# Summing every second product of the first level by accumulating DMA, and a third place for B

## The reference

```python
x = x + conv_block(_gn(x))    # L0: each image makes its own 7x7 depthwise filters
x = x + ssm_block(_gn(x))     # L1: three levels of a state space model, both directions

def _ssm(x, ...):             # per level and direction, n = 16 states
    dA  = exp(delta[..., None] * A)
    dBx = delta[..., None] * Bs[:, :, None, :] * xt[..., None]
    h = h * dA + dBx                     # a scan over positions, per channel and state
    y = sum over states of h * C, + xt * Dv
    return layernorm(y, g, b)            # over the 128 channels
```

## Time and profile before

| | us |
|---|---|
| median of 3 runs | 4344.43 |
| lowest, highest | 4341.24, 4347.71 |
| the profiled execution | 4338.19 |
| its span | 4336.4 |

### The profile page before, as it was taken

How to read it: one execution, slowest core, us unless ns; L and a number is a source line. 1 busy time by engine, 2 the same in 40 slices (tenths; PEclk the granted TensorE clock), 3 DMA queues, 4 the chain that set the end, 5 groups by cost and what they waited for, 6 DMA issues and landing times.

```text
span 4336.4 us, 51200 instructions
## 1 busy us (share of the span) xinstructions
PE 3086.1 (71%) x11852; PEld 1449.5 (33%) x11852; DVE 3559.6 (82%) x4199; ACT 2552.1 (59%) x6006; POOL 3338.1 (77%) x1908
## 2 busy tenths in 40 slices
PE   6977767777776778767777876777877777876511
PEld 3433333333332433333333333333333333332200
DVE  2178888888888888888888888888888888898777
ACT  4466665655665665666656666665676566565432
POOL 0069597895969879696896969789596996969798
PEclk8988788888888888887888888888887888888755
DMA  1036354463544446354453534446253454635444
GB/s 40 1 125 206 117 179 147 157 200 108 197 140 157 165 147 204 115 190 146 157 186 125 201 129 167 149 159 209 99 196 131 168 174 137 205 113 182 165 157 174
DMA packets 187260, 663.95 MB, mean 153 GB/s; under 512 B 22736, under 2 KB 24672, under 8 KB 186976
## 3 DMA queue, kind: packets, MB, share of 16 engines
q1 hardware_dynamic: 186976, 661.47, 45.0%
HBM read 639.76 MB, written 21.63 MB: 153 GB/s over the span
## 4 chain that ended last, share of the span: by engine, by line
POOL 28%; issue 23%; DVE 17%; PE 13%; ACT 11%; DMA 6%; DVEq 1%; POOLq 1%; SPq 0%; ACTq 0%
POOL bx L1342 12%; POOL y L1370 7%; DMA bb<-bc_rows 6%; DVE h L581 6%; POOL h L1365 5%; ACT diag L1085 5%; PE pconv L822 4%; DVE slot_c L572 3%; POOL bx L1345 2%; PE pm L848 2%; DVE rs L528 1%; DVE rs L520 1%; ACT slot_b L1200 1%; PE pm L839 1%; POOL delta L1310 1%
## 5 line engine op out<-in xcount | busy, mean ns | idle before, releaser
L822 PE MATMUL pconv<-pad,diag 128*128 128x512 f16 x8064 | 2052.6, 412 | 132.7 <-DVE xn L506 66.9
L1370 POOL TENSOR_TENSOR y<-y,h 128x1024 f32<-128x1024 f32 (+2 forms) x672 | 1335.6, 1987 | 153.9 <-DVE h L581 131.2
L1200 ACT ACTIVATE slot_b<-delta,nega 128x512 f32<-128x512 f32 (+1 forms) x1280 | 804.3, 640 | 1010.6 <-DVE slot_c L572 1009.0
L822 PEld LDWEIGHTS pconv<-pad,diag 128*128 128x128 f16 x8064 | 826.1, 104 | 1328.6 <-issue 423.3
L1342 POOL TENSOR_TENSOR bx<-bb,u 128x1024 f32<-128x1024 f32 x512 | 1219.4, 2382 | 19.9 <-DMA bb<-bc_rows 19.9
L572 DVE TENSOR_TENSOR_SCAN slot_c<-slot_b,bx 128x512 f32<-128x512 f32 (+1 forms) x1024 | 954.2, 956 | 296.1 <-POOL bx L1342 255.4
L581 DVE TENSOR_TENSOR h<-slot_c,cb 128x512 f32<-128x512 f32 x1280 | 860.4, 673 | 36.6 <-POOL y L1370 36.6
L572 DVE TENSOR_TENSOR_SCAN slot_c<-slot_b,slot_c,bx 128x512 f32<-128x512 f32 x512 | 663.7, 1296 | 74.8 <-ACT slot_b L1200 18.7
L1310 POOL TENSOR_TENSOR delta<-delta,rs 128x512 f32<-128x512 f32 (+1 forms) x96 | 111.8, 1164 | 464.6 <-DVE rs L530 464.6
L1365 POOL TENSOR_TENSOR h<-h 128x512 f32<-128x512 f32 (+3 forms) x384 | 361.2, 941 | 98.3 <-DVE h L551 80.7
L1085 ACT ACTIVATE diag<-id,chi 128x128 f16<-128x128 f16 x1344 | 426.6, 386 | 10.7 <-PE pconv L822 10.1
(11 more groups left out here) (168 smaller groups left out, 3555.2 us busy)
## 6 DMA issues: line engine op xcount, KB each, us to landing
bb<-bc_rows SPq DMA_DIRECT2D x592, 512.0 KB, 4.5
cb<-bc_rows SPq DMA_DIRECT2D x592, 512.0 KB, 4.4
xr<-in_x SPq DMA_DIRECT2D x16, 1024.0 KB, 4.9
out<-ob SPq DMA_DIRECT2D x16, 1024.0 KB
bc_rows<-rows SPq DMA_DIRECT2D x64, 64.0 KB, 1.6
w<-in_w SPq DMA_DIRECT2D x2, 256.0 KB
wc<-in_wc SPq DMA_DIRECT2D x2, 256.0 KB
bc_rows<-rows SPq DMA_DIRECT2D x16, 32.0 KB, 1.5
```

What stands on the lines that cost most here:

```text
L822: ins = nc.tensor.matmul(bank(pconv, k), w, pad[:, t, part, rows:rows + 16, dx:dx + W], start=first and m == 0, stop=last and m == 2)
L1200: ins = nc.scalar.activation(slot_b[:, o:o + w], delta[:, so + c:so + c + w], ACT.Exp, scale=nega[:, st, n0 + n:n0 + n + 1])
L1370: pool.tensor_tensor(yv, yv, src[:, 0] if len(src.shape) == 3 else src, ALU.add).then_inc(q_y.sem, 1)
```

## The change

In the first level every second product, those of units with odd n (8 per direction, 16 per image), is no longer summed by a POOL instruction. POOL issues a DMA instead, from the product's place in `h` to `ob[:, d]`: a plain copy for the first of a direction (n = 1), an accumulating one (`accum_op=ALU.add`) for the others. Each waits for the one before. `ob`, the tile of the output, serves as the second sum; POOL waits before the first of an image until the store of the last image's result has read it, and the wait for this on DVE (in `output`) goes. `q_y` counts only the sums that stay, a new semaphore `q_acc` counts the DMAs, and who waited for `q_y` waits for the one that applies. In `norm_centre` of the first level's halves PE adds up both sums: a second matmul with `cen` on `ob` into the same PSUM.

B's ring gets a third place (4 KB of a partition), `get_b` goes three units ahead instead of two, with a third load in the bridge, and `dynamic_dma_scratch_size` is halved to 4096.

```diff
-BR, CR = 2, 3
+BR, CR = 3, 3
+def by_dma(q):
+    u, _ = PRODUCTS[q]
+    return UNITS[u][0] == 1 and UNITS[u][3] % 2 == 1
+def added(q):
+    return sum(not by_dma(v) for v in range(q))
+def sent(q):
+    return sum(by_dma(v) for v in range(q))
...
+        pool_held = sem("pool_held")
-        q_y = Count("q_y", NP)
+        q_y = Count("q_y", added(NP))
+        q_acc = Count("q_acc", 16 * sent(NP))
...
+                    if k + 3 < NU:
+                        get_b(i, k + 3)
                     if k + 2 < NU:
-                        get_b(i, k + 2)
                         get_c(i, k + 2)
...
                     for k in range(2):
                         get_b(j, k)
                         get_c(j, k)
+                    get_b(j, 2)
...
                 if p == 0 and q >= HR:
-                    dve.wait_ge(q_y.sem, q_y.at(i, q - HR + 1))
+                    if by_dma(q - HR):
+                        dve.wait_ge(q_acc.sem, q_acc.at(i, 16 * sent(q - HR + 1)))
+                    else:
+                        dve.wait_ge(q_y.sem, q_y.at(i, added(q - HR + 1)))
...
             def output(i, hh):
-                if hh == 0:
-                    dve.wait_ge(ob_free.sem, ob_free.at(i + 1, 0))
...
-                pe.wait_ge(q_y.sem, q_y.at(i, NORM_NEEDS[k]))
+                pe.wait_ge(q_y.sem, q_y.at(i, added(NORM_NEEDS[k])))
                 o = norm_psum(k)[0][:, 0:cols]
                 if d == 2:
                     o = o.rearrange("p (d n) -> p d n", d=2)
-                nc.tensor.matmul(o, cen[:, :], src, start=True, stop=True).then_inc(n_yc.sem, 1)
+                    nc.tensor.matmul(o, cen[:, :], src, start=True, stop=True).then_inc(n_yc.sem, 1)
+                    return
+                pe.wait_ge(q_acc.sem, q_acc.at(i, 16 * sent(NORM_NEEDS[k])))
+                nc.tensor.matmul(o, cen[:, :], src, start=True, stop=False)
+                nc.tensor.matmul(o, cen[:, :], ob[:, d, c0:c0 + n], start=False, stop=True).then_inc(n_yc.sem, 1)
...
+                if by_dma(q):
+                    pool.wait_ge(q_pr.sem, q_pr.at(i, weighed(q)))
+                    pool.sem_inc(pool_held, 1)
+                    if sent(q) == 0:
+                        pool.wait_ge(ob_free.sem, ob_free.at(i + 1, 0))
+                        pool.sem_inc(pool_held, 1)
+                        pool.dma_start(ob[:, d, :], h[:, q % HR, 0:ln]).then_inc(q_acc.sem, 16)
+                    else:
+                        pool.wait_ge(q_acc.sem, q_acc.at(i, 16 * sent(q)))
+                        pool.sem_inc(pool_held, 1)
+                        if UNITS[k][3] == 1:
+                            pool.dma_start(ob[:, d, :], h[:, q % HR, 0:ln]).then_inc(q_acc.sem, 16)
+                        else:
+                            pool.dma_start(ob[:, d, :], h[:, q % HR, 0:ln], accum_op=ALU.add).then_inc(q_acc.sem, 16)
+                    return
...
-                    pool.wait_ge(q_y.sem, q_y.at(i, q))
+                    pool.wait_ge(q_y.sem, q_y.at(i, added(q)))
...
-    nc = bacc.Bacc(..., dynamic_dma_scratch_size=8192)
+    nc = bacc.Bacc(..., dynamic_dma_scratch_size=4096)
```

More of the change, by code:

```diff
@@ L1511 @@
     arrays = {n: np.ascontiguousarray(v) for n, v in arrays.items()}
-    nc = bacc.Bacc("TRN2", target_bir_lowering=False, num_devices=1, dynamic_dma_scratch_size=8192)
+    nc = bacc.Bacc("TRN2", target_bir_lowering=False, num_devices=1, dynamic_dma_scratch_size=4096)
     aps = {n: nc.dram_tensor("in_" + n, v.shape, mybir.dt.from_np(v.dtype), kind="ExternalInput").ap() for n, v in arrays.items()}
```

## The result

| | median us | lowest to highest | ratio to before, 95% |
|---|---|---|---|
| before | 4342.77 (5 runs) | 4331.35 to 4347.71 | |
| changed | 4367.55 (5 runs) | 4361.57 to 4370.38 | 1.0064 [1.0046, 1.0083] |

The changed kernel is slower by 0.64%, some 28 us. Its profiled execution took 4366.67 us, with a span of 4364.9. The forecast was 4282 and "faster"; the range of 4230 to 4480 holds the time, the sign is wrong.

A forecast was written before the change was run, and what follows sets the result against it. The prediction took POOL to set the pace in the late first level, with DVE's floor next. 4338.2 - 104 (first level) + 42 (bridge matmuls) = 4276, with 6.2 to the median 4282; range 4230 to 4480.

The forecast's parts named there:

- What bounds the kernel, and the relief: Late first level: POOL sets the pace; relieved, units 4.1 apart, `bx` wait 255 to some 150, gain 6.5 a body.
- the sum: Whole kernel: 4338.2 - 104 (first level) + 42 (bridge) = 4276, plus 6.2 to the median: 4282.
- Issue on POOL: POOL's queue, first level: issuing a DMA costs 1.3 us, the middle between 0.32 and 2.35; two units 8.23.
- Landing: First-level DMAs into `ob` land in 6 us, hidden by 1 to 2 us only; some 8 are allowed.
- signs of being wrong: POOL's issue over 1.9, L581 or POOL waiting for `ob` to land, or B and C loads landing over 7 us.
- Issuing is dear: POOL's odd first-level units: each further us of issue costs 7 a body; 4386 at 2.3, 4465 at 3; chance 0.16.
- the cheap issue: POOL, first level: at 0.32 us an issue, gain 9.4 a body, bridge 2.0, giving 4226; chance 0.10.
- The landing comes too late for the ring of three products: DVE's weighing L581, every second unit: decides from 8 us landing (about 4380); 4522 at 9; chance 0.16.
- It cancels: Whole kernel: issue near 1.9 or a landing of some 7.5 leaves the time at 4344; chance 0.10.
- DMA engines full: First level: accumulating DMAs occupy the engines twice as long, units 4.5 apart, giving 4367; chance 0.08.
- Centre matmuls in the bridge: Norms 4 and 5: two more matmuls cost 2.0 to 3.7, taken as 2.6 a body, 42 us.
- Third place of B: B's ring: cover against short loads at 4.1 a unit, worth nothing alone; in the bridge nothing.

The follow-up runs named there:

- number 1: Kernel before with its 16 odd first-level sums left out and nothing in their place: 4192.11 us, 0.9675.
- experiment 3: Changed kernel whose accumulating DMAs read `xc` instead of `h`, so DVE need not wait for their landing: 4292.78 us, 0.9891 to before.
- experiment 2: Changed kernel with every accumulating DMA made a plain copy of the same size, second sum left out: 4286.20 us, 0.9876 to before.
- number 13: Changed kernel with four product places, direction 1's last two odd sums on POOL, `ob` merged into `y` there, scratch 2048, `dg` on ACT: 4224.39 us, 0.9744 to before.
- experiment 4: Changed kernel without the second centre matmul, the sums in `ob` left out of the norm: 4341.88 us, 1.0006 to before.
- number 5: Kernel before with only B's third place, loads three units ahead and half the scratch: 4340.63 us, 1.0006.
- number 6: Changed kernel with two places for B and loads two units ahead: 4346.84 us, 1.0017 to before.
- number 8: Changed kernel with the small product `dg` made by ACT instead of DVE: 4310.65 us, 0.9945 to before.

## Why the prediction was wrong

**What bounds the kernel, and the relief: right.** POOL's pace was the limit between units 10 and 33, and number 1 shows what its relief can bring, 9.0 a body. The wait for `bx` ends at 94.2, where some 150 was forecast; in that stage 6.65 a body went, for 5.5 of the sum, and the early units won 2.5 for its 1.0. The units from 18 to 30 were forecast 4.1 apart. Where nothing else holds DVE up they are 3.85 apart (2490.54, 2494.39, 2498.24), DVE's floor, but from 18 to 30 the mean of bodies 2 to 14 is 4.68, against 4.72 before: what `bx` gave back, the landing, `fi` and `dg` took.

**Issue on POOL: right mechanism, too dear.** 1.3 was taken. An accumulating issue lasts 0.88 and a copy 0.59; from the start of one to the start of the product behind it, it is 0.61 (2472.52 and 2473.13). By that two units cost POOL 3 x 2.31 + 0.61 = 7.5, less than DVE's 7.7, so POOL leaves no wait in plain units. The rival *Issuing is dear* falls. That of the cheap issue was nearer with its price of 0.32 and gave 4226; the gain that it named was there in the wait for `bx` and was taken by the next points.

**Landing: the step that failed.** "I take 6", "It is hidden, by 1 to 2 us only", and "L581 with no wait for a DMA". It is 7.6 in the median and up to 12.0, 8.1 between units 18 and 30, and 8.5 to 9.6 for the three products that DVE mostly waits for. L604 waits 48 times for it, 49.0 us in all, and POOL 90.8; both were named as signs of being wrong. By experiments 3 and 2 DVE's wait is worth 75 to 82 us, which alone turns 4282 into some 4360, and with it the sign. The room of "some 8" was right: from the issue at 2500.98 to the end of DVE's second scan of unit 27 it is 8.2. What was mis-sized is the landing, and that one figure stood for all 16 of a body. The rival *The landing comes too late for the ring of three products* had the place right, and the mechanism. Its price was for a landing of 9 us at every second unit, where it is so late at three of them; and its 4380 for 8 us doesn't follow from its own rule, by which nothing is lost up to 8. The case *It cancels* names the landing measured, "of some 7.5", and 4344. Both stood in the text with 0.16 and 0.10, and the row beside them, loads of 6.0 and 7.0 in traffic, spoke for them: even plain copies in its place take 6.5 (experiment 2). The estimate took 6, and the room was 6.6 to 8.

**DMA engines full: the right number for the wrong reason.** That rival gave 4367, and 4367.55 came, which is luck. Its premise holds: queue 0 is 14.7% of the span for 256 DMAs, 2.5 us of the 16 engines each, and as copies 7.7% of 4278 us, 1.3 each. With 1.3 for the 32 plain ones among the 256, an accumulating one comes to 2.7, an estimate. The Trainium skill (Collectives: The Full Stack, The bandwidth ceiling) says of a reduce over several cores that its add in the DMA needs two source reads and that this halves its rate; the trace agrees, with 2.7 against 1.3. The engines come near to full as well: 0.92 of the time between units 18 and 30 (2464.60 to 2519.90), 0.66 before. But they don't hold the units to 4.5: experiment 3 keeps every byte of that traffic and is 75 us faster, and number 13, with the same DMAs in these units, runs them 4.26 apart. What the double occupancy does is lengthen the landing, 6.5 to 7.6. The loads of B beside it took 4.6 before, in units 18 to 30, and in the same units of the changed kernel:

```profile
bb<-bc_rows SPq DMA_DIRECT2D x13, 512.0 KB, 6.2
...
ob<-h POOLq DMA_DIRECT2D x7, 512.0 KB, 8.1
```

That is under the 7 that the prediction named as its limit. With plain copies (2414 to 2469 there) B takes 6.2 too and `ob` 7.4, so what lengthens the loads of B is the further DMA, not that it accumulates.

**Centre matmuls in the bridge: mis-sized.** 42 us was forecast, 25 measured by experiment 4 (1.6 a body for 2.6).

**Third place of B: right in "cover" and in "worth nothing alone", wrong in "nothing" for the bridge.** Alone it is 1.0006. As cover it is worth 36 to 49 us, once `dg` is out of the way. In the bridge it isn't free: three taps of DVE ran beside one `bx` before, and now beside two, that of unit 2 too. First the changed kernel, then the kernel before:

```profile
2595.93 7.68 DVE L518 SCALAR_TENSOR_TENSOR u<-xh,wmid,u 128x928 f32<-128x928 f32 x3
```

```profile
2308.73 5.58 DVE L498 SCALAR_TENSOR_TENSOR u<-xh,wmid,u 128x928 f32<-128x928 f32 x3
```

```profile
2596.24 6.37 POOL L1370 TENSOR_TENSOR bx<-bb,u 128x1024 f32<-128x1024 f32 x2
```

The last stage of a body is 10.33 in the changed kernel and in number 5, 9.65 in number 6 and 9.25 before.

**The small product: not seen.** No step of the sum speaks of DVE's L477. It is a single instruction, 0.24 us by itself and 0.64 in the kernel before, that met the whole of POOL's `bx` and cost 52 us in this order, with what waits for it on PE.

Put together, from number 1 to the changed kernel 169 us are lost. The parts taken away one by one give 75 to 82 (landing), 52 (`dg`) and 25 (matmuls), 152 to 159 in all. They overlap, since what one wait ends can uncover another (numbers 3 and 8 both shorten the wait at `fi`), so the sum is no proof that nothing is missing; issue, traffic and the last stage were not taken apart.

## What to carry to other kernels

Work that goes from an engine to a DMA is not gone: it comes back as a latency at whoever reuses the source buffer. Size the ring for the landing of that transfer in that traffic, at the place where the consumer runs fastest, with the slowest transfer seen there as the floor, not with the median of plain loads. Compare two traces unit by unit, not at the same time of the span. When a faster engine changes the order in which two engines meet, look at the smallest instructions too: compare each line's median length before and after, since a longer one shows up there before any list of waits names it. Take an unexpected sign, here a spare buffer that did harm, as a pointer to such a meeting and not as the buffer's price.

## What the runs showed of the hardware

An accumulating DMA of 512 KB from SBUF to SBUF took 2.7 us of the 16 engines (an estimate, see above) against 1.3 for the copy, 0.88 against 0.59 us on POOL to issue, and 7.6 against 6.5 us to land.

A DVE product of 49x49 elements took 0.24 us in one order, and 3.06 where it met POOL's 128x1024 product, ending with it. In the changed kernel and numbers 2 to 4, bodies with POOL's work beside it, `dg` was so held 49 times of 56, for 2.6 to 3.2 us: each time POOL's issue of a DMA had begun 0.22 to 0.41 us ahead of it and `bx` was recorded 0.20 to 0.38 behind its start. In the other 7 the issue had begun 0.14 ahead at most, `bx` came later, and `dg` took 0.24. The scans of DVE beside such an operation kept their length; here DVE's and POOL's time lines of the changed kernel, four us earlier:

```profile
2468.45 1.23 DVE L592 TENSOR_TENSOR_SCAN slot_c<-slot_b,bx 128x512 f32<-128x512 f32 x1
```

```profile
2467.35 2.65 POOL L1411 TENSOR_TENSOR y<-y,h 128x1024 f32<-128x1024 f32 x1
```

Three taps (L518), with two inputs in SBUF, took 7.68 beside two `bx` and 5.58 beside one. By itself a tap takes 1.2; the one that meets a `bx` takes 3.3, and that `bx` 3.2 instead of 2.35.

The Trainium skill (SBUF — State Buffer, Who interferes with whom) says that a DVE instruction with at most one input in SBUF doesn't contend with POOL outside the modes that use both ports, and one with two inputs there does. It says too that a `tensor_scalar` can enter such a mode and that then whichever engine issues first holds the shared ports for its whole instruction. The trace agrees in all three: 1.23, 7.68 and 3.06 us. One thing stays open: `dg` is recorded 0.37 us ahead of POOL's product and still ended with it; POOL's issue of the DMA (2472.52 to 2473.40) lay over the start of both. Number 1 issues no DMA from POOL, and there `dg` was held once, by a `bx` recorded 0.03 behind it, and not by those 0.11 behind and more. With the small product on ACT (number 8) that meeting is gone, and the kernel is 52 us faster.

The list of waits put 49.0 us to the landing; without that wait the kernel was 75 us faster.
